# Attention on one core: two maximum tiles reduced as one, and every other tile sent through the score banks

## The reference

```
x1 = x + LN(attn(LN(x)));   out = x1 + LN(ffn(LN(x1)))
attn: q, k, v = x Wq + bq, x Wk + bk, x Wv + bv      16 heads of 64
      scores  = q k^T / 8;  p = softmax(scores);  ctx = p v
      y = x + ctx Wo + bo;  LN(y) * gamma + beta
ffn:  (silu(x Wg) * (x Wu)) Wd                        hidden width 768
```

## Time and profile before

| what | value |
|---|---|
| median of three runs | 3201.6 us (3199.45 to 3202.89) |
| the profiled execution's own time | 3200.07 us |
| its span, first to last instruction | 3198.3 us |
| granted TensorE clock over the span | 0.974 |
| busy: PE, DVE, ACT, POOL | 92%, 82%, 75%, 72% |
| first prologue, to the first exponential | 141 us |
| head 20 (steady) | 79.1 us for its 64 steps |
| feed-forward | from about 2720 us |

### The profile page before, as it was taken

One profiled execution on the slowest core, in us unless ns is written; L12 is line 12 of the kernel. 1 busy time (PEld: TensorE's weight loads), 2 busy tenths in 40 slices (PEclk: granted clock), 3 DMA queues, 4 the chain that ended last, 5 costly groups with the idle time before them and its releaser, 6 DMA issues. The chain is left out here.

```text
span 3198.3 us, 83116 instructions
## 1 busy us (share of the span) xinstructions
PE 2949.4 (92%) x33632; PEld 2129.6 (67%) x33632; DVE 2638.3 (82%) x4729; ACT 2390.4 (75%) x4587; POOL 2296.0 (72%) x1810
## 2 busy tenths in 40 slices
PE   5799999999999999968999999999999999788897
PEld 4466666666666666656666666666666666577775
DVE  5688888888888888866888888888888888488886
ACT  3588888888888888945888888888888889633322
POOL 4488888888888888845888888888888888513222
PEclk8899999999999999978999999999999999899998
DMA  3523222222222333115233333233333222212110
GB/s 102 142 60 65 63 63 63 63 63 63 63 63 63 64 65 91 24 52 155 49 65 64 66 65 66 63 66 66 65 67 65 64 61 68 80 66 73 53 40 20
DMA packets 211660, 214.04 MB, mean 67 GB/s; under 512 B 158672, under 2 KB 181328, under 8 KB 198992
## 3 DMA queue, kind: packets, MB, share of 16 engines
q1 hardware_dynamic: 211280, 208.79, 27.7%
HBM read 53.16 MB, written 37.88 MB: 28 GB/s over the span
## 5 line engine op out<-in xcount | busy, mean ns | idle before, releaser
L474 POOL TENSOR_TENSOR p_l<-p_f,p_h 128x512 f16<-128x512 f32 x1536 | 1926.0, 1275 | 423.0 <-ACT p_h L539 418.9
L586 DVE TENSOR_REDUCE mx<-ps_aux 128x1 f32<-128x512 f32 x2048 | 1351.5, 681 | 313.3 <-PE ps_aux L754 311.4
L538 ACT ACTIVATE p_f<-ps_score 128x512 f32<-128x512 f32 x2048 | 1288.6, 630 | 109.9 <-PE ps_score L767 71.5
L539 ACT ACTIVATE p_h<-ps_score 128x512 f16<-128x512 f32 x2048 | 1299.2, 635 | 0.0
L766 PE MATMUL ps_score<-q_hilo,k_hihi 128*128 128x512 f32 x2048 | 1193.7, 583 | 0.3 <-ACT p_h L539 0.3
L787 PEld LDWEIGHTS ps_ctx<-v_hi_one_lo,p_h 128*128 128x128 f16 x8192 | 747.3, 96 | 285.7 <-issue 270.9
L754 PE MATMUL ps_aux<-k_half,q_half 65*128 65x512 f16 x2048 | 813.0, 398 | 103.7 <-DVE mx L586 97.5
L787 PE MATMUL ps_ctx<-v_hi_one_lo,p_h 128*128 128x65 f16 x8192 | 872.0, 194 | 1.5 <-POOL p_l L474 1.4
L789 PE MATMUL ps_ctx<-v_hi_one_lo,p_h 128*128 128x64 f16 x8192 | 862.2, 195 | 0.0
L791 PE MATMUL ps_ctx<-v_hi_one_lo,p_l 128*128 128x65 f16 x8192 | 856.8, 192 | 0.0
L767 PE MATMUL ps_score<-q_hi_max,k_lo_one 65*128 65x512 f32 x2048 | 816.0, 398 | 0.0
(11 more groups left out here) (126 smaller groups left out, 2624.5 us busy)
## 6 DMA issues: line engine op xcount, KB each, us to landing
k_hihi<-hi_st SPq DMA_DIRECT2D x64, 512.0 KB, 8.7
v_heads<-v_new SPq DMA_DIRECT2D x64, 258.0 KB, 2.0
v_hi_one_lo<-v_heads SPq DMA_DIRECT2D x32, 516.0 KB, 9.4
q_hilo<-hi_st SPq DMA_DIRECT2D x32, 512.0 KB, 4.8
q_hilo<-lo_st SPq DMA_DIRECT2D x32, 512.0 KB, 6.6
q_hi_max<-hi_st SPq DMA_DIRECT2D x32, 512.0 KB, 4.6
k_lo_one<-lo_st SPq DMA_DIRECT2D x32, 512.0 KB, 6.7
heads<-ctx_n SPq DMA_DIRECT2D x128, 128.0 KB, 2.0
```

The source lines that it names most:

```text
L474: nc.gpsimd.tensor_tensor(p_l[:, r], p_f[:, r], p_h[:, r], ALU.subtract).then_inc(lo_pool, 1)
L538: nc.scalar.activation(p_f[:, r], ps_score[:, bank], ACT.Exp, scale=K ** -0.5)
L539: nc.scalar.activation(p_h[:, r], ps_score[:, bank], ACT.Exp, scale=K ** -0.5).then_inc(exp_done, 1)
L586: nc.vector.reduce_max(mx[:, blk % 2, tt, ch:ch + 1], ps_aux[:, bank], AX_X).then_inc(max_read, 1)
```

## The change

The two maximum tiles of a pair of steps are made first, back to back, into the two banks of `ps_max`, and one DVE reduction over [128, 2, 512] reads both. `ps_max` holds one pair: PE may write the next one when the reduction is done (`max_read`). Chunks and turned tiles leave these banks and take slots of the 4 score banks, in one common ring (`ring_plan`, `take_slot`). Chunks sit at steps 32, 40, 48 and 56 in place of 35, 41, 51 and 57. ACT takes a chunk 5 steps later, POOL's part comes 7 steps later. In `weigh` the order of the three matmuls is reversed for every second group of queries.

```diff
-CHUNKS_AT = (3, 9)
-TAKE_LAG = 4
+CHUNKS_AT = (32, 40, 48, 56)
+TAKE_LAG = 5
+LOW_CHUNK_LAG = 7
...
-        ps_aux = ctx.enter_context(nc.psum_tensor("ps_aux", [P, 2, BLK], F32))
+        ps_max = ctx.enter_context(nc.psum_tensor("ps_max", [P, 2, BLK], F32))
...
-            k, rest = divmod(t - 2 * KT, 7)
+            k, rest = divmod(t - 2 * KT, 6)
...
+        def ring_plan(u, last, coming):
+            _, chunks, turns = side_items(u, last, coming)
+            slot = {("score", t): t % RING for t in range(AHEAD)}
+            for t in range(0, STEPS, 2):
+                new = [("score", t + AHEAD + k) for k in range(2)]
...
+                new += [("chunk", c) for c in chunks[t]] + [("turn", *item) for item in turns[t]]
+                for item in new:
+                    slot[item] = len(slot) % RING
...
-                    for chunk, _ in chunks[t - AHEAD] if t >= AHEAD else ():
+                    for chunk in chunks[t - LOW_CHUNK_LAG] if t >= LOW_CHUNK_LAG else ():
                         low_chunk(g + u + 2, chunk)
...
-                dve.wait_ge(aux_full, n + 1)
-                nc.vector.reduce_max(mx[:, blk % 2, tt, ch:ch + 1], ps_aux[:, bank], AX_X).then_inc(max_read, 1)
-                if kt == KT - 1:
+                dve.wait_ge(max_full, n + 1)
+                nc.vector.reduce_max(mx[:, blk % 2, tt, ch:ch + 2], ps_max[:, :, :], AX_X).then_inc(max_read, 1)
+                if kt == KT - 2:
...
+            def take_slot(sem, value):
+                if len(ring) == RING:
+                    pe.wait_ge(*ring.pop(0))
+                ring.append((sem, value))
...
+            def max_pair(u, g, blk, kt, n):
...
+                pe.wait_ge(max_read, n + 1)
+                q = qM[u][:, blk * BLK:(blk + 1) * BLK].rearrange("k (p t) -> k t p", t=TB)[:, tt]
+                for h in range(2):
+                    mm = nc.tensor.matmul(ps_max[:, h], q, kM[u][:, (ch + h) * BLK:(ch + h + 1) * BLK],
+                                          start=True, stop=True)
+                mm.then_inc(max_full, 1)
...
+                    parts = [(acc, p_h, v_one), (acc[:, 0:K], p_h, v_lo), (acc, p_l, v_one)]
+                    if q % 2:
+                        parts.reverse()
...
+                for t in range(0, STEPS, 2):
+                    for ahead, blk, k in maxima[t]:
+                        max_pair((u + ahead) % 2, g + u + ahead, blk, k, (g + u) * PAIRS + KT + t // 2)
+                    for n in (t + AHEAD, t + AHEAD + 1):
+                        if n < STEPS:
+                            score(u, g + u, n, slot["score", n])
+                        elif not (last and u == 1):
+                            score(1 - u, g + u + 1, n - STEPS, slot["score", n])
+                    for chunk in chunks[t]:
+                        project(g + u + 2, chunk, slot["chunk", chunk])
...
+                    weigh(u, g, t)
+                    weigh(u, g, t + 1)
```

More of the change, by code:

```diff
@@ L259, in prologue_items @@
                 order.append(("value", k, 0))
-                if k >= rest[0] + 8:
-                    order += [("max", *next(maxima)) for _ in range(2 if opening else 1)]
+                if k >= rest[0] + 8 and (opening or k % 2):
+                    order.append(("max", *next(maxima)))
             left = list(maxima)
@@ L288, in side_items @@
                 if not (last and u == 1 and ahead):
[L289 to L293, removed]
-                if coming and u == 1 and norm_at(t - 4) is not None:
[L295 to L298, removed]
+                    maxima[t].append((ahead, (j + 2) % NB, kt))
+                if not last and t in CHUNKS_AT:
+                    chunks[t].append(CHUNKS_AT.index(t))
+                if coming and u == 1 and norm_at(t - 4) is not None:
+                    turns[t] += [(norm_at(t - 4), c) for c in range(DT)]
+            return maxima, chunks, turns
+        def ring_plan(u, last, coming):
[3 more added lines that the diff above has]
+                new = [("score", t + AHEAD + k) for k in range(2)]
+                if last and u == 1:
+                    new = [item for item in new if item[1] < STEPS]
+                new += [("chunk", c) for c in chunks[t]] + [("turn", *item) for item in turns[t]]
+                for item in new:
+                    slot[item] = len(slot) % RING
+            assert (last and u == 1) or all(slot["score", STEPS + t] == t % RING for t in range(AHEAD))
+            return slot
         def walk(eng, prologue, head):
@@ L307, in pair @@
                 def pair(i, first, last):
-                    g = snap(eng, b * H + i)
-                    n = 0
                     for u in range(2):
-                        n = head(b, i, g, u, first, last, more and last, n)
+                        head(b, i, b * H + i, u, first, last, more and last)
                 for k in range(HH):
@@ L402, in load_for_feed_forward, with head @@
                     .then_inc(wo_loaded, 16)
-            def head(b, i, g, u, first, last, coming, n):
+            def head(b, i, g, u, first, last, coming):
                 if last and u == 1 and not coming:
@@ L466, in prologue, with head @@
                         low_chunk(b * H + a, c)
-            def head(b, i, g, u, first, last, coming, n):
-                _, chunks, turns, n = side_items(u, last, coming, n)
+            def head(b, i, g, u, first, last, coming):
+                _, chunks, _ = side_items(u, last, coming)
                 for t in range(STEPS):
@@ new lines, in head @@
+            def head(b, i, g, u, first, last, coming):
+                maxima, chunks, turns = side_items(u, last, coming)
+                slot = ring_plan(u, last, coming)
+                for t in range(0, STEPS, 2):
+                    for ahead, blk, k in maxima[t]:
[5 more added lines that the diff above has]
+                            score(1 - u, g + u + 1, n - STEPS, slot["score", n])
+                    for chunk in chunks[t]:
+                        project(g + u + 2, chunk, slot["chunk", chunk])
+                    for gr, c in turns[t]:
@@ L856, in head @@
                                                      x_all[:, gr, k, c * P:(c + 1) * P], ident[:, :])
-                        mm.then_inc(aux_full, 1)
-                    if t + AHEAD < STEPS:
-                        score(u, g + u, t + AHEAD)
-                    elif not (last and u == 1):
-                        score(1 - u, g + u + 1, t + AHEAD - STEPS)
-                    if t % 2:
-                        for chunk, number in chunks[t]:
-                            project(g + u + 2, chunk, number % 2)
-                        weigh(u, g, t - 1)
-                        weigh(u, g, t)
```

186 lines of the change are left out of this document (79 added, 107 removed).

## The result

The changed kernel takes 3227.97 us (3227.57 to 3229.36) against 3200.52 for the kernel before on the same chip: ratio 1.0087, 95% interval 1.0069 to 1.0104. It is slower, by 27 us; 3228 was forecast. The first view is the page: span, and the groups that answer to the earlier trace rows.

The account below looks back on a forecast made before the run. PE was taken to bound the kernel, with its waits nearly all for the DVE reduction that frees the maximum banks. The terms -75 + 104 - 3 = +26 us gave 3226 on the profiled execution, 3228 on the median; range 3120 to 3290.

Parts of the forecast that it names:

- two large terms: Steady heads: -75 us for the blocks without chunks and +104 us for those with chunks.
- Wide reduction: DVE's read of both maximum banks: 1.14 us start to start, 1.26 from start to PE's release.
- Half with chunks: Second half of steady heads: PE stalls 1.50 us a chunk behind DVE's low part and casts, +104 us over 112 chunks.
- slot wait of step 41: Behind a chunk, step 41's score waits 0.3 us for step 38's exponential to free its ring slot, inside the 1.50.
- Half without chunks: Blocks without chunks: PE never waits, a block falls from 18.38 to 17.28 us, -75 us over 68 blocks.
- PE's floor: PE's time for a pair of steps without waits: 2.16 us, so 17.28 a block without chunks, 20.04 with two.
- Weighing order: Reversed order of the weighing matmuls in every second group: -3 us, bounds 13 us either way.
- Prologues: Prologues: DVE, ACT and POOL pass each chunk along as before, so 0 us.
- Rival 1: Behind a chunk, casts meet an idle POOL: 3132 us, or 3075 with the low part unblocked too; chance 0.30.
- Rival 2: The cycle without chunks doesn't fit: low part takes 1.5 us, -10 in place of -75, 3293 us; chance 0.12.
- Rival 3: In steady heads the waits only move: a head keeps its 79.1 us, 3202 within 6 us; chance 0.06.

Follow-up runs that it names:

- e6: The changed kernel with POOL's low parts of steps t % 8 of 6 and 7, in each head's second half, over 16 of 512 columns: 3113.06 us, ratio 0.9734.
- e1: The changed kernel with the three weighing matmuls always in their old order: 3231.89 us, ratio 1.0108.
- e2: The kernel before with only the reversed weighing order added: 3197.01 us against 3196.87, ratio 1.0000.
- e8: The changed kernel with PE waiting, before each of the second head's prologue chunks, until the maximum pairs made so far are read: 3246.24 us, ratio 1.0154.
- e4: The changed kernel with ACT taking a chunk 7 steps later in place of 5: 3060.5 us, ratio 0.9570.

## Why the prediction was right

The time, 3228, came out to the microsecond; that much is luck, since three terms were off (by +14, +3 and -16 us) and nearly cancelled. The direction and the two large terms rest on the mechanism, which the runs bear out.

- *Wide reduction* (1.14 start to start, 1.26 to PE's release): measured 1.14 and 1.27 (mean duration 1220 ns). Right.
- *Half with chunks* (+104): measured +104.0. The mechanism is as put: low part blocked by POOL's operation, POOL's next ahead of the first cast, the second cast free. Low 5.33 to 6.53, first cast ending 7.84, PE released at 9.36 were worked out; the trace, counted from the chunk pair's start, has the same within 0.1. The slot wait of step 41, put at 0.3 and inside the 1.50, measured 0.43, with 1.13 left for DVE, 1.56 together. That is 0.06 more than worked out, and the floor of eight steps was 9.93 where 10.02 was taken, so 11.51 for 11.52 is partly luck. e6 shows that POOL's hold makes the 1.13.
- *Half without chunks* (-75 with the four other heads): -47.4 - 13.3 = -61. Pairs do run at PE's floor, so the step holds and the size is off by two terms that I had covered with "sit in a gap of about 0.8". The negation at a head's end stands ahead of the next read and in the gap that also holds a low part; the kernel's order on DVE showed that, and it costs 0.70 a head. The weight split costs 0.2 to 0.3.
- *PE's floor*: taken as unchanged at 2.16; it is 2.13 with both tiles first, some 0.9 us a head at most, partly absorbed in waits. Not foreseen.
- *Weighing order* (-3): 0 within the measurement, both ways round (e1, e2).
- *Prologues* (0): -15.9. The step failed: "DVE, ACT and POOL pass each chunk along as before" left out that PE had waited too. Before, a chunk needed one of two banks, free only when the maxima ahead of it were read; with such a wait put back (e8) the 10 us of the second prologue return. The granted clock, lower there in both runs in which PE waits so, was not thought of either; its share is open.

Rival 1 (casts meet an idle POOL) did not come, but its prices were right where it was brought about: with neither blocked a stall of 0.13 a chunk was worked out, and e4 has 0.07. Rival 2 needed a low part of 1.5 without chunks; its median there is 1.19 (30 of 196 took 1.5 or more). Rival 3 is out: the two halves moved by 1.7 down and 3.7 up.

## What to carry to other kernels

When two buffers that were freed singly become one buffer freed at once, write down every loop through it and every operation of the reader that falls between two reads; its slack, not the reader's total work, says whether it is faster. When an engine waits out of order for a late input (ACT before the chunk), look at what it delays, and what those delayed operations then collide with: moving the taking behind two exponentials gave 5.2% here, against a change that by itself cost 0.9%. And a bank shared by two kinds of work ties their chains together, which cost up to 10 us in the second prologue here, a part of it at a lower clock.

## What the runs showed of the hardware

- DVE's low parts, casts and negations exclude POOL's subtractions by whole instructions, and the two alternate. In the changed kernel 61 of 128 negations over four columns took 0.92 to 1.13 us and 64 took 0.15 or 0.16; the one at 1842.46 (1.13) ended with the operation of POOL that it met (1843.57), the one at 1878.79 (0.16) met none. DVE's reduction from PSUM kept its 1.21 to 1.23 us.
- A reduction from PSUM of [128, 2, 512] took 1220 ns where two of 512 columns take 0.61 start to start each; the width saves 0.08 us.
- Six 512-column matmuls take 0.03 us less when the two float16 ones stand together than when they alternate with the scores (pairs of 2.13 and 2.16); which part of the alternation costs this was not separated.
